# Three edits in a fused eight-stage kernel: sparse contexts in one series, local tokens copied by VectorE, global query projection behind the contexts

## The reference, cut to what matters

```python
# sparse attention (once): 16 heads of 8, only the 10 highest-scored queries per head, of which u are valid
scores = einsum('bhud,bhld->bhul', Q_sparse, K) / sqrt(DK)      # 160 rows x 2048 keys
attn = softmax(scores); out = einsum('bhul,bhld->bhud', attn, V)
valid = arange(10) < u; full = zeros.at[scatter_idx].set(out, mode='drop'); return full @ Wo.T + bo
# local layers (twice, each call DEPTH = 2 layers): shift_token, qkv, l2norm, rotary, windowed attention, gated MLP
h = shift_token(x); q, k, v = split(h @ wqkv, 3); ...; x = x + o @ wo
h = shift_token(x); h = layernorm(h) * lg + lb; a, g = split(h @ w1 + b1, 2); x = x + (a * gelu(g)) @ w2 + b2
# global grouped attention (once): 16 query heads of 64 over 4 key heads, 2048 x 2048 scores per head, rotary positions
```

## Time and profile before

| what | value |
|---|---|
| median of 3 runs | 3734.76 us (3733.58 to 3739.41) |
| the profiled execution | 3737.75 us, span 3736.0 us |
| granted TensorE clock, mean | 0.943 of full |
| busy share of the span | PE 87%, PEld 53%, DVE 71%, ACT 52%, POOL 45% |
| last block of sparse | 1295 to 1368 us |
| first local stage | 1370 to 1797 us |
| global stage | 1797 to 3303 us |
| second local stage | 3305 to 3736 us |

### The profile page before, as it was taken

The page is one execution under the profiler, slowest core; times in us unless marked ns, Lnnn a source line. Parts: engine busy times, 40 slices in busy tenths (PEclk is TensorE's granted clock), DMA queues, the critical chain, the costliest instruction groups (busy, mean ns, idle before and its releaser), DMA issues. The chain is left out here.

```text
span 3736.0 us, 70352 instructions
## 1 busy us (share of the span) xinstructions
PE 3254.7 (87%) x27870; PEld 1992.5 (53%) x27870; DVE 2669.1 (71%) x4726; ACT 1946.8 (52%) x3456; POOL 1687.1 (45%) x1133
## 2 busy tenths in 40 slices
PE   5999999999747368998699999999999999969997
PEld 3667777777636256777333333333333333337776
DVE  4667667676655857777677777787778777667776
ACT  2445444444423219999344444444444444439997
POOL 0121212121114226665166666666666666756664
PEclk8999999999968669999799999999999999979999
DMA  2000000000010010000100000000000000010000
GB/s 95 2 1 2 2 2 1 2 2 2 2 54 2 6 55 1 2 2 2 30 1 1 1 1 1 1 1 1 1 1 1 1 1 1 1 46 2 2 2 13
DMA packets 22482, 31.76 MB, mean 8 GB/s; under 512 B 8610, under 2 KB 18252, under 8 KB 20940
## 3 DMA queue, kind: packets, MB, share of 16 engines
q1 hardware_dynamic: 22156, 27.26, 2.2%
HBM read 26.20 MB, written 1.05 MB: 7 GB/s over the span
## 5 line engine op out<-in xcount | busy, mean ns | idle before, releaser
L3190 POOL TENSOR_TENSOR global_acc_pool<-global_acc_pool,global_probs 128x1024 f32<-128x1024 f32 x320 | 796.6, 2489 | 246.3 <-ACT global_probs L3131 222.3
L3131 ACT ACTIVATE global_probs<-global_ps 128x1024 f32<-128x1024 f32 x512 | 519.9, 1024 | 626.6 <-PE global_ps L2986 611.2
L3257 DVE TENSOR_REDUCE global_part<-global_ps 128x2 f32<-128x1024 f32 x512 | 622.7, 1218 | 304.3 <-PE global_ps L2968 304.1
L2986 PE MATMUL global_ps<-global_q,global_k 64*128 64x512 f32 x2048 | 529.8, 595 | 0.0
L2997 PE MATMUL global_ps<-global_probs,global_v 128*64 128x512 f32 x2048 | 495.7, 605 | 0.0
L970 POOL TENSOR_TENSOR delta_etm<-delta_et,C_tile 128x1024 f32<-128x1024 f32 x16 | 40.2, 2514 | 755.6 <-ACT delta_et L853 755.6
L2968 PE MATMUL global_ps<-global_khh,global_qhh 64*128 64x512 f32 x1024 | 307.1, 597 | 59.0 <-DVE global_part L3257 52.0
L2984 PE MATMUL global_ps<-global_mrow,global_first 64*128 64x512 f32 x1024 | 321.1, 624 | 0.0
L2968 PEld LDWEIGHTS global_ps<-global_khh,global_qhh 64*128 64x128 f32 x1024 | 97.2, 187 | 375.9 <-DVE global_part L3257 300.5
L2997 PEld LDWEIGHTS global_ps<-global_probs,global_v 128*64 128x64 f32 x2048 | 124.2, 136 | 266.0 <-issue 178.2
L1071 DVE COPY_PREDICATED delta_Yd<-delta_tri,delta_ps 64x512 f32<-64x512 uint32 x160 | 116.6, 729 | 191.3 <-PE delta_ps L587 188.8
(11 more groups left out here) (584 smaller groups left out, 7090.5 us busy)
## 6 DMA issues: line engine op xcount, KB each, us to landing
delta_cw<-in_conv_taps SPq DMA_DIRECT2D x4, 1024.0 KB, 10.6
local_tab<-in_rot_tables SPq DMA_DIRECT2D x2, 2048.0 KB, 12.4
local_tab<-in_rot_tables SPq DMA_DIRECT2D x2, 1536.0 KB, 7.7
localw_wqkv<-in_L_ffn_wqkv SPq DMA_DIRECT2D x2, 768.0 KB
delta_wqkvz<-in_L_attn_a_W_qkvz SPq DMA_DIRECT2D x1, 1024.0 KB, 5.6
local_tab<-in_rot_tables SPq DMA_DIRECT2D x2, 512.0 KB, 4.2
global_cos<-in_rope_cos SPq DMA_DIRECT2D x8, 128.0 KB, 3.3
global_sin<-in_rope_sin SPq DMA_DIRECT2D x8, 128.0 KB, 3.3
```

Of the source, the lines that this page charges most:

```text
L2986: mm = pe.matmul(ps[:, 2 * (at % 2) + s, :], k2[own, group_of(u) % 2, P * k:P * k + P], q[own, u % 3, :], start=False, stop=True)
L3131: act.activation(probs[:, at % RING, :], ps[:, 2 * (at % 2):2 * (at % 2) + 2, :].rearrange("p b n -> p (b n)"), ACT.Exp).then_inc(S["probs ...
L3190: ins = eng.tensor_tensor(sums[:, u % 2, :], sums[:, u % 2, :], probs[:, at % RING, :], ALU.add)
L3257: dve.tensor_reduce(part[:, u % 2, r % SLOTS, :], ps[:, rough_banks(r), :], X_AXIS, ALU.max)\
```

## The change

In sparse, probabilities are no longer scaled: the row weight (validity over sum) is applied by ScalarE when it copies out the 80 output rows. TensorE turns both halves first, then makes one series of contexts with 160 columns, and VectorE masks all heads at once. In local, `keep_tokens` moves from ScalarE to VectorE, at the end of a slot, and the slots begin at -4. In global, the query projection moves from the head of slice 0 to behind that slice's contexts, without a wait of its own; the swap and rotation move to slice 1, the joining to slice 2; and `place_max` goes ahead of the joining of keys.

```diff
 # sparse, TensorE
-                    pe.wait_ge(A["probs_ready"], g + 1)
+                    pe.wait_ge(A["probs_exp"], g + 1)
...
-                def contexts(g):
-                    pe.wait_ge(A["probsT_ready"], g + 1)
+                def contexts():
+                    pe.wait_ge(A["probsT_ready"], 2)
                     for t in range(TILES):
-                        mm = pe.matmul(ps[:, 4 * g + 3, 0:HALF], v_all[:, t, :], probsT[:, g, t, :],
+                        mm = pe.matmul(ps[:, 7, 0:H * TOP], v_all[:, t, :], probsT[:, :, t, :],
                                        start=(t == 0), stop=(t == TILES - 1))
...
                 turn_probs(0)
-                contexts(0)
                 turn_probs(1)
-                contexts(1)
+                contexts()
 # sparse, ScalarE
+                    act.wait_ge(A["weights_ready"], g + 1)
+                    act.activation(ow[:, g, :], ps[0:HALF, 5 + g, 0:DIM], ACT.Copy, scale=srow[:, g:g + 1]).then_inc(A["ow_ready"], 1)
 # sparse, VectorE
-                    dve.tensor_scalar(probs[:, g, :], probs[:, g, :], own, None, ALU.mult).then_inc(A["probs_ready"], 1)
...
-                scale_probs(0)
-                scale_probs(1)
                 keep_probs(0)
                 keep_probs(1)
-                own_heads(0)
-                own_heads(1)
+                row_weights(0)
+                row_weights(1)
+                dve.wait_ge(A["o_ps"], 1)
+                dve.tensor_tensor(oT[:], heads(ps[:, 7, 0:H * TOP], H), over_inner(hm, TOP), ALU.mult)\
+                    .then_inc(A["oT_ready"], 1)
 # local
-        SLOTS = range(-3, ITEMS + 7)
+        SLOTS = range(-4, ITEMS + 7)
-                def keep_tokens(m):
-                    t = m % TILES
-                    act.wait_ge(S["xT_ps"], m + 1)
-                    act.activation(hT[UP, tokens(t)], ps[UP, TURN, 0:P], ACT.Copy)
-                    act.activation(hT[DOWN, P * t + 1:P * t + P + 1], ps[DOWN, TURN, 0:P], ACT.Copy)\
-                        .then_inc(S["hT_ready"], 1)
...
+                def keep_tokens(m):
+                    t = m % TILES
+                    dve.wait_ge(S["xT_ps"], m + 1)
+                    dve.tensor_copy(hT[UP, tokens(t)], ps[UP, TURN, 0:P])
+                    dve.tensor_copy(hT[DOWN, P * t + 1:P * t + P + 1], ps[DOWN, TURN, 0:P])\
+                        .then_inc(S["hT_ready"], 1)
...
                         row_stats(n - 2)
+                    if valid(n + 4):
+                        keep_tokens(n + 4)
 # global, TensorE
-                        if j == 0 and u + 2 < UNITS:
-                            pe.wait_ge(S["mrow_ready"], u + 1)
-                            project(pe, ("q", u + 2))
...
                         if j == 2 and u:
                             out_sums(pe, u - 1)
+                        if j == 0 and u + 2 < UNITS:
+                            project(pe, ("q", u + 2))
 # global, ScalarE
-                        if j == 0 and u + 2 < UNITS:
+                        if j == 1 and u + 2 < UNITS:
                             swap_halves(("q", u + 2))
 # global, VectorE
-                        if j == 0 and u + 2 < UNITS:
+                        if j == 1 and u + 2 < UNITS:
                             rotate(("q", u + 2))
-                        if j == 1 and u + 2 < UNITS:
+                        if j == 2 and u + 2 < UNITS:
                             join_rotated(("q", u + 2))
...
+                        if j == 7 and u + 1 < UNITS:
+                            place_max(u + 1)
                         if j == 7 and next_keys(u):
                             join_rotated(next_keys(u))
-                        if j == 7 and u + 1 < UNITS:
-                            place_max(u + 1)
```

More of the change, by code:

```diff
@@ L2066, in sparse_attention @@
         A = signals(nc, ctx, """z_ready idx_ps idx_ready cols_ps cols_ready sel_ready gather_ps qexp_ready total_ready nmean_ready
-            spread_ready u_ready top_scores_ps rowmax_ready probs_exp probs_ready probsT_ps probsT_ready o_ps oT_ready ow_ps
+            spread_ready u_ready top_scores_ps rowmax_ready probs_exp weights_ready probsT_ps probsT_ready o_ps oT_ready ow_ps
             ow_ready selT_ready y_ps top_step""")
@@ L2110, in rows_out @@
                 def rows_out(g):
-                    pe.wait_ge(A["oT_ready"], g + 1)
+                    pe.wait_ge(A["oT_ready"], 1)
                     pe.matmul(ps[0:HALF, 5 + g, 0:DIM], oT[:, 8 * g:8 * g + 8, :].rearrange("p h r -> p (h r)"),
@@ L2143, in _ @@
                     act.wait_ge(A["ow_ps"], g + 1)
-                    act.activation(ow[:, g, :], ps[0:HALF, 5 + g, 0:DIM], ACT.Copy).then_inc(A["ow_ready"], 1)
+                    act.wait_ge(A["weights_ready"], g + 1)
+                    act.activation(ow[:, g, :], ps[0:HALF, 5 + g, 0:DIM], ACT.Copy, scale=srow[:, g:g + 1]).then_inc(A["ow_ready"], 1)
             @block.gpsimd
@@ L2197, in _, with row_weights @@
                     dve.tensor_scalar(own, own, -SCALE, None, ALU.mult).then_inc(A["rowmax_ready"], 1)
-                def scale_probs(g):
+                def row_weights(g):
                     dve.wait_ge(A["probs_exp"], g + 1)
@@ L2202, in scale_probs @@
                     link(dve.reciprocal(own, own))
-                    link(dve.tensor_tensor(own, own, valid[:], ALU.mult))
-                    dve.tensor_scalar(probs[:, g, :], probs[:, g, :], own, None, ALU.mult).then_inc(A["probs_ready"], 1)
+                    dve.tensor_tensor(own, own, valid[:], ALU.mult).then_inc(A["weights_ready"], 1)
                 def keep_probs(g):
@@ L2211, in keep_probs @@
                     ins.then_inc(A["probsT_ready"], 1)
-                def own_heads(g):
-                    dve.wait_ge(A["o_ps"], g + 1)
-                    own = slice(8 * g, 8 * g + 8)
-                    dve.tensor_tensor(oT[:, own, :], heads(ps[:, 4 * g + 3, 0:HALF], 8), over_inner(hm[:, own], TOP), ALU.mult)\
-                        .then_inc(A["oT_ready"], 1)
-                scale_probs(0)
-                scale_probs(1)
                 keep_probs(0)
                 keep_probs(1)
-                own_heads(0)
-                own_heads(1)
+                row_weights(0)
[3 more added lines that the diff above has]
+                    .then_inc(A["oT_ready"], 1)
                 dve.wait_ge(S["bias_added"], 1)
@@ L2581, in _ @@
                         gelu(n - 4)
-                    if valid(n + 3):
-                        keep_tokens(n + 3)
                     if valid(n - 2):
```

## The result

The changed kernel takes 3643.1 us (median of 4, 3635.5 to 3644.4), the kernel before 3736.9 on the same chip: ratio 0.9745, 95% interval 0.9731 to 0.976. It is 93.8 us faster. The prediction was 54 us (3681, range 3660 to 3710): right in sign and in most steps, outside its range in size.

A forecast was written before the change was run, and what follows sets the result against it. No engine bounds the whole: ScalarE limits steady local, a serial chain with TensorE at half clock the last sparse block, TensorE global. Gains of 13 sparse, 7 local and 34 global sum to 54 us: 3734.8 - 54 = 3681, range 3660 to 3710.

The forecast's parts named there:

- I take 11.1 and 2 us of a scatter that begins fast: Sparse: 11.1 us gained with the gather's clock in the series, plus 2 from the scatter, giving 13 us.
- the bound of 18: Sparse, upper bound: the scatter starts at full clock, keeps it and halves, 7 us more than 11.1.
- 21 + 9 = 30: Global, units with keys: 21 us from 12 boundaries at 1.75, 9 from six clock falls of 1.5 us.
- rest of the extra idle: Global, units with keys: 0.6 us more idle in the next slices, where VectorE is behind, taken as gone.
- I take 0.2 in 18 units, 4 us; bounds -0.4 and +0.8: Global, plain units: gain from moving the projection's work, 4 us in all, with ends of -7 and +14.
- the 2.25 us sum: Global, plain units: VectorE's sum of tile 15, colliding with GpSimd; no longer behind a rotation, uncollided near 1.21 us.
- The context's wait: Global, plain units: `keep_context` falls behind the swap, so the unit's first context comes some 0.35 us too early for it.
- All the idle there is to win is 1.18 per unit: Global, plain units: ceiling on the gain, from TensorE's 43.30 us per unit with 42.12 of them busy.
- C: Rival: clock helps more, sparse 18, all plain-unit idle gone, global 44; 3666, or 3658 with local at 15; chance 0.10.
- B: Rival: global gives 8 instead of 34, as the clock falls at other idles and rough scores wait; 3707, chance 0.18.
- E: Rival: no difference; global's gains fail (-2), local loses 5, sparse gives 9; 3733, chance 0.04.
- D: Rival: slower; GpSimd shuts out the join in slice 2, about 1.0 us per collision; 3756 at 2.5 per unit, chance 0.04.

The follow-up runs named there:

- run 7: The kernel after, with the sparse contexts as two series of 80 columns back to back instead of one of 160; 3650.8 us.
- run 12: The kernel after once more, unchanged, on the same chip as three others; 3641.6 us, ratio 0.9754.
- run 3: The kernel before with one edit: in slice 7 of global VectorE places the maxima ahead of the joining of the keys; 3708.6 us.
- Run 4: The kernel before with the whole global part, except that the keys are still joined ahead of the placed maxima; 3693.0 us.
- Runs 13: The kernel before with VectorE's rotation moved to slice 1 and joining to slice 2; swap and projection stay in slice 0; 3728.3 us.
- run 15: The kernel before with VectorE's rotation moved to slice 1, joining to slice 2, and also ScalarE's swap moved from slice 0 to slice 1; 3703.2 us.
- run 8: The kernel after, with ScalarE copying the finished context ahead of the swap in global and VectorE copying the first three token tiles early in local; 3639.7 us.
- run 9: The kernel of run 8 with the joining of the queries moved from slice 2 to slice 4 and the rounding copy from 3 to 5; 3628.7 us.
- runs 11: The kernel of run 8 with the joining at the end of slice 2 and the rounding copy still at the head of slice 3; 3694.6 us.
- run 14: The kernel of run 9 with the inversion of the sums ahead of the first reduction of slice 3; 3736.7 us, ratio 1.0002 to before.
- runs 5: The kernel before with one line changed: the joining of the query rotation moves from slice 1 to slice 2; 3730.6 us.

## Why the prediction was right or wrong

*Sparse, predicted 13, measured 17.8.* Start of the series (1333.68, measured 1333.71), its length (6.7 to 8.6, 6.97) and the 1.7 us behind it (1.57) were right. The step that failed is "I take 11.1 and 2 us of a scatter that begins fast": the mechanism stood in the bound of 18, and the scatter took it in full, 6.6 us. The fast series and the fast scatter go together: run 7, without the one, has not the other.

*Local, predicted 7, measured 7.2, and 16 alone.* The slot came to 11.46 to 11.50 (11.48 predicted), the exponents' wait to 0.22 (0.2 to 0.3), the late start to 4.4 per stage (4.45), with 0.5 more to the first squares (0.9). That the sum also fits is partly luck: the clock in drain and prologue moves it by up to 5 us, and run 12 gives 6.4 by the same marks.

*Global, the maxima first: predicted 21 + 9 = 30, measured 28.2 alone.* Right: the wait is gone and the clock falls are gone. But the two smaller terms did not come: no rough score waits 0.55 behind the boundary (run 3), and the "rest of the extra idle" of 0.6 stayed. They cancel, 1.6 us a boundary where 1.75 was predicted, and that is luck. The prediction also counted the falls by one too many: of the twelve units with keys five ran at 0.96 to 0.97, and the sixth fall was in a plain unit right behind one (44.62 us).

*Global, the plain units: predicted 4, measured 40.* This is the failed step, "I take 0.2 in 18 units, 4 us; bounds -0.4 and +0.8". Two faults lie in it. First, the number of units: the move works in all 30 units that project. The sum left out the 12 with keys, and it priced the first unit as a plain one, where it is worth 4.6 us. Run 4 gives 4.5 for the first, 19.5 for the twelve (part of it clock), and the rest, 18.5, for the plain ones. Second, the size: 1.0 a unit, not 0.2. The prediction saw the 2.25 us sum and that it collides; but it named the rotation ahead of it and offset it with the context's wait. Runs 13 and 15 show another cause: the swap ahead of the first exponents made GpSimd late enough to collide, 0.85 us per unit, and moving the rotation without it gave nothing. The context's wait did come (0.35), and cost less than it shows: run 8 took it away and gained nothing, since VectorE's queue in slices 2 to 4 was next.

The ceiling, "All the idle there is to win is 1.18 per unit", is not one. TensorE's busy time fell by 0.44 with the same instructions, and run 9 shortened the unit by 1.27 in all, more than the 1.18. Ends of matmuls are modelled, so a stall can be booked as a longer matmul.

*The rivals.* C was nearest in mechanism (a fuller clock in sparse, all idle of plain units) and still 23 us short, 15 with its larger local term, since it too moved only the plain units. B and E are refuted by run 3 and by the result: no clock fell at another idle. (It did in runs 11 and 14, whose rough scores wait 1.7 and 3.0 us.) D's price is real in size, about 0.9 us per collision, but its sign here was a gain: a collision was removed in slice 1, and the joining in slice 2 (1.93 us long in after) costs at most the 0.3 that run 9 got back.

*Still open:* why the clock in the first local stage's drain differs, even between two executions of one kernel; no run isolates it.

## What to carry to other kernels

When work is moved between slices, ask of each engine's queue what now starts earlier or later on the other engines, and whether two that exclude each other will meet: here one swap of 2.4 us on an engine half idle decided 0.85 us per unit, and one inversion moved ahead of one reduction cost 108 us. Count the units in which an edit works before you price it, and take a wait or a pitch of starts, not span minus busy, as the ceiling of what TensorE can win. A wait that is removed pays only if the next one in the ring is later: after runs 5 and 8 the same queue had moved most of its stall to a later rough score, and of the 0.55 us that run 9 went for it got 0.27. And repeat the kernel before a gain of a few us is put down to an edit: stages that were not touched differed by 4 to 6 us.

## What the hardware showed that was not expected

- Two instructions of 80 columns cost more than one of 160. At half clock (0.50) their starts were 0.21 us apart in run 7, those of 160 columns 0.27 in after. Both series stand without a gap and start at half clock, yet it stayed at half through 64 of the narrow ones (13.94 us) and rose within 32 of the wide ones (6.97 us in all). The scatter behind them, the same 64 instructions, took 7.41 us at full clock instead of 14.02 at half.
- A VectorE copy with a single SBUF input was held as well beside GpSimd: the inversion's copy of 512 columns took 0.43 us in run 9 and 1.55 in run 14. In both it ended 0.29 us behind the end of one of GpSimd's additions, which it had met near its end in run 9 and in its middle in run 14.
- The clock in the drain of the first local stage and global's prologue is no property of the kernel. From the end of the scatter to the first placed maxima the whole change took 481.4 us in one execution and 478.0 in another (run 12); in the last 100 us of it the granted clock was 0.77 and 0.81. With the old order of local it was 483.9 before and 479.5 in run 15, which differs from before in global alone. Readings of this stretch carry up to 5 us that no edit explains.
